# A fused attention and feed-forward block: q, k and v of the self-attention from three float32r products in place of one in fp32

## What is computed

```python
def _L0_attn_ref(x, w_qkv, b_qkv, w_out, b_out):
    B, T, C = x.shape                      # 64, 64, 256
    qkv = x @ w_qkv + b_qkv                # w_qkv is 256 x 768
    q, k, v = jnp.split(qkv, 3, axis=-1)
    ...
    att = jnp.einsum('bhqd,bhkd->bhqk', q, k) / jnp.sqrt(jnp.float32(D_HEAD))
    att = jnp.where(causal, att, -jnp.inf)
    att = jax.nn.softmax(att, axis=-1)
    y = jnp.einsum('bhqk,bhkd->bhqd', att, v)
    ...
    return y @ w_out + b_out

x = x + _L0_xattn_ref(_layernorm(x), ctx_1024, ctx_1024, ...)
x = x + _L0_attn_ref(_layernorm(x), w_qkv, b_qkv, w_out, b_out)
x = x + _L0_ffn_ref(_layernorm(x), w_gate, w_up, w_down)
```

## Time and profile before

| | |
|---|---|
| median of 3 runs | 1038.72 us (1038.37 to 1040.5) |
| the profiled execution | 1037.98 us |
| its span, first to last instruction | 1036.2 us |
| mean granted clock of PE | 0.98 |
| busy: PE, DVE, ACT, POOL | 89%, 80%, 70%, 37% |

### The profile page before, as it was taken

The page is one execution under the profiler, slowest core; times in us unless marked ns, Lnnn a source line. Parts: engine busy times, 40 slices in busy tenths (PEclk is TensorE's granted clock), DMA queues, the critical chain, the costliest instruction groups (busy, mean ns, idle before and its releaser), DMA issues. The chain is left out here.

```text
span 1036.2 us, 30640 instructions
## 1 busy us (share of the span) xinstructions
PE 919.6 (89%) x9794; PEld 737.1 (71%) x9794; DVE 831.3 (80%) x1810; ACT 728.0 (70%) x2061; POOL 386.4 (37%) x420
## 2 busy tenths in 40 slices
PE   4999999999999999999998799999999666666666
PEld 4888888888888888888887586777777433443444
DVE  4778787878787878787877588888888779999995
ACT  3676767676767676767676577767667378888886
POOL 2223232323232323232322445554554245445543
PEclk9899999999999999999999999999999779999999
DMA  8111111111111111111110000000000000000000
GB/s 278 43 35 40 35 40 35 40 35 40 35 40 35 40 35 40 35 40 35 40 35 1 2 2 1 0 0 0 0 0 1 1 1 21 25 20 20 20 25 31
DMA packets 31591, 31.36 MB, mean 30 GB/s; under 512 B 3280, under 2 KB 30800, under 8 KB 31568
## 3 DMA queue, kind: packets, MB, share of 16 engines
q1 hardware_dynamic: 30720, 30.73, 9.6%
q10 hardware_dynamic: 848, 0.33, 0.1%
HBM read 26.86 MB, written 4.19 MB: 30 GB/s over the span
## 5 line engine op out<-in xcount | busy, mean ns | idle before, releaser
L470 ACT ACTIVATE probs<-psum,nmax 128x256 f32<-128x256 f32 x512 | 237.6, 487 | 99.6 <-DVE nmax L430 99.6
L430 DVE TENSOR_REDUCE nmax<-psum 128x2 f32<-128x512 f32 x256 | 159.0, 684 | 31.0 <-PE psum L301 31.0
L478 POOL TENSOR_TENSOR rstd<-vare,minus_half 128x1 f32<-128x1 f32 x96 | 52.8, 550 | 337.0 <-DVE vare L368 337.0
L314 PE MATMUL psum<-id_sb,probs 128*128 128x128 f32 x1024 | 137.8, 278 | 10.5 <-ACT probs L470 8.9
L314 PEld LDWEIGHTS psum<-id_sb,probs 128*128 128x128 f32 x1024 | 113.8, 142 | 26.0 <-ACT probs L470 26.0
L487 POOL TENSOR_TENSOR cl<-c_sb,ch 128x512 fp32r<-128x512 f32 x64 | 81.2, 1269 | 104.3 <-ACT ch L445 104.3
L470 ACT ACTIVATION_READ_ACCUMULATOR probs<-psum,nmax 128x1 f32 x512 | 112.2, 219 | 0.0
L451 ACT ACTIVATE probsT<-psum 128x512 f32<-128x512 f32 x160 | 90.2, 608 | 13.5 <-PE psum L314 11.4
L494 POOL TENSOR_TENSOR rm<-rinv,hm_sb 128x256 f32<-128x256 f32 x64 | 39.8, 622 | 133.9 <-DVE rinv L407 133.9
L906 POOL TENSOR_TENSOR probs<-probs,silu 128x512 f32<-128x512 f32 x64 | 81.2, 1291 | 7.2 <-ACT probs L899 7.2
L378 DVE TENSOR_TENSOR v_sb<-psum,bv_sb 128x512 f32<-128x512 f32 x64 | 44.3, 692 | 39.6 <-PE psum L285 39.6
(11 more groups left out here) (117 smaller groups left out, 2318.2 us busy)
## 6 DMA issues: line engine op xcount, KB each, us to landing
c_sb<-in_ctx_t SPq DMA_DIRECT2D x64, 256.0 KB, 2.7
x_sb<-in_x SPq DMA_DIRECT2D x32, 128.0 KB, 2.1
out<-y_sb SPq DMA_DIRECT2D x32, 128.0 KB, 1.7
w_raw<-in_w_gate SPq DMA_DIRECT2D x1, 1024.0 KB, 7.9
w_raw<-in_w_up SPq DMA_DIRECT2D x1, 1024.0 KB, 10.0
w_raw<-in_w_down SPq DMA_DIRECT2D x1, 1024.0 KB, 12.5
wqkv_sb<-in_w_qkv SPq DMA_DIRECT2D x1, 768.0 KB, 6.5
wq_sb<-in_wq ACTq DMA_DIRECT2D x1, 256.0 KB, 4.2
```

The lines of the kernel that those rows point to most:

```text
L314: last = nc.tensor.transpose(sp[g][:, c:c + P], probs[:, 2 * g + u, kh * P:(kh + 1) * P], id_sb[:])
L430: nc.vector.tensor_reduce(nmax[:, 2 * g:2 * g + 2], sp[g].rearrange("p (u s) -> p u s", u=2), AX.X, ALU.max, negate=True).then_inc(max_don ...
L470: nc.scalar.activation(probs[:, j, :], sp[g][:, u * S:(u + 1) * S], ACT.Exp, bias=nmax[:, j:j + 1], accum_out=rsum[:, j:j + 1]).then_inc(e ...
```

## The change

The three float32r products replace the fp32 ones. The weights are split once, near the end of the cross-attention block: `wqkvh` by an ACT copy, `wqkvl` by a DVE subtraction. Each tile's transposed rows are split as they leave PSUM: ACT writes `xh` (in place of `xnT`, same shape), then DVE writes `xl`, PSUM less `xh`. `pe_qkv2` waits for `xl_done` and issues, for q and k, 24 matmuls in place of 8, and for v six in place of two. The next `pe_xt2` waits until `xl` has been read out of PSUM, the writing of `xh` and `xl` until the projections of the tile before are done (`v2_mm`).

Three things are moved or put in between. On PE `pe_xt2` of t + 3 goes from behind `pe_out2` to ahead of `pe_r2`. On ACT `act_xt2` goes from behind `act_r2` to ahead of it. On DVE `dve_xl` of t + 3 stands between `dve_sub2` and `dve_y2`.

```diff
@@ -78,7 +78,13 @@
         bk_sb = sb("bk_sb", [P, KT])
         bv_sb = sb("bv_sb", [P, D])
         bo_sb = sb("bo_sb", [P, D])
+
+
         wqkv_sb = sb("wqkv_sb", [P, KT, 3 * D])
+        wqkvh = sb("wqkvh", [P, KT, 3 * D], F32R)
+        wqkvl = sb("wqkvl", [P, KT, 3 * D], F32R)
+        xh = sb("xh", [P, KT, P], F32R)
+        xl = sb("xl", [P, KT, P], F32R)
         bqk_sb = sb("bqk_sb", [P, 2 * KT])
         bv2_sb = sb("bv2_sb", [P, D])
         wout_sb = sb("wout_sb", [P, KT, D])
@@ -514,7 +520,10 @@
         rstd2_done = sem("rstd2_done")
         xn2_done = sem("xn2_done")
         xt2_mm = sem("xt2_mm")
-        xt2_ev = sem("xt2_ev")
+        w2h_split = sem("w2h_split")
+        w2l_split = sem("w2l_split")
+        xh_done = sem("xh_done")
+        xl_done = sem("xl_done")
         qk_mm = sem("qk_mm")
         qk_ev = sem("qk_ev")
         v2_mm = sem("v2_mm")
@@ -595,21 +604,25 @@
         def pe_xt2(pe, t):
             pe.wait_ge(xn2_done, t + 1)
             pe.wait_ge(v2b_done, t)
+            pe.wait_ge(xl_done, t)
             for k in range(KT):
                 last = nc.tensor.transpose(xq_ps[:, k, :], xn[:, k * P:(k + 1) * P], id_sb[:])
             last.then_inc(xt2_mm, 1)
 
         def pe_qkv2(pe, t):
-            pe.wait_ge(xt2_ev, t + 1)
+            pe.wait_ge(xl_done, t + 1)
             pe.wait_ge(qk_ev, t * 4)
             for m in range(2 * KT):
+                cols = slice(m * P, (m + 1) * P)
+                for n, (w, x) in enumerate(((wqkvh, xh), (wqkvh, xl), (wqkvl, xh))):
+                    for k in range(KT):
+                        last = nc.tensor.matmul(qk_ps[:, m, :], w[:, k, cols], x[:, k, :],
+                                                start=n + k == 0, stop=n == 2 and k == KT - 1)
+            last.then_inc(qk_mm, 1)
+            for n, (x, w) in enumerate(((xh, wqkvh), (xh, wqkvl), (xl, wqkvh))):
                 for k in range(KT):
-                    last = nc.tensor.matmul(qk_ps[:, m, :], wqkv_sb[:, k, m * P:(m + 1) * P],
-                                            xnT[:, k, :], start=k == 0, stop=k == KT - 1)
-            last.then_inc(qk_mm, 1)
-            for k in range(KT):
-                last = nc.tensor.matmul(v2_ps, xnT[:, k, :], wqkv_sb[:, k, 2 * D:3 * D],
-                                        start=k == 0, stop=k == KT - 1)
+                    last = nc.tensor.matmul(v2_ps, x[:, k, :], w[:, k, 2 * D:3 * D],
+                                            start=n + k == 0, stop=n == 2 and k == KT - 1)
             last.then_inc(v2_mm, 1)
 
         def pe_scores2(pe, t, par):
@@ -678,6 +691,12 @@
 
         both = s_both.rearrange("p (a b) -> p a b", b=L)
 
+        def dve_xl(v, t):
+            v.wait_ge(xh_done, t + 1)
+            v.wait_ge(v2_mm, t)
+            nc.vector.tensor_tensor(xl[:], xq_ps, xh[:].bitcast(F32),
+                                    ALU.subtract).then_inc(xl_done, 1)
+
         def dve_max2(v, t):
             v.wait_ge(s2_mm, t + 1)
             nc.vector.tensor_reduce(nmax2[:], both, AX.X, ALU.max).then_inc(max2_done, 1)
@@ -717,7 +736,8 @@
 
         def act_xt2(a, t):
             a.wait_ge(xt2_mm, t + 1)
-            nc.scalar.activation(xnT[:], xq_ps, ACT.Copy).then_inc(xt2_ev, 1)
+            a.wait_ge(v2_mm, t)
+            nc.scalar.activation(xh[:], xq_ps, ACT.Copy).then_inc(xh_done, 1)
 
         def act_qk(a, t, par):
             a.wait_ge(qk_mm, t + 1)
@@ -1030,6 +1050,7 @@
                 body(NT - 1, False, True)
                 pe.wait_ge(w2_in, 16 * len(SET2))
                 pe.wait_ge(r_ev, NT * 2)
+                pe.wait_ge(w2l_split, 1)
                 pe_qkv2(pe, 0)
                 pe_out(pe, NT - 1, True)
 
@@ -1072,6 +1093,10 @@
                         v.wait_ge(y_ev, 1)
                         dve_stats(v, LN2, 0, at(0))
                         dve_xn(v, LN2, 0, at(0), xt2_mm)
+                    if last:
+                        v.wait_ge(w2h_split, 1)
+                        nc.vector.tensor_tensor(wqkvl[:], wqkv_sb[:], wqkvh[:].bitcast(F32),
+                                                ALU.subtract).then_inc(w2l_split, 1)
                     if not last:
                         dve_q(v, t + 1)
                     dve_o(v, t, 0)
@@ -1087,6 +1112,7 @@
                 with v.Fori(1, NT - 1) as t:
                     body(t, False, False)
                 body(NT - 1, False, True)
+                dve_xl(v, 0)
                 v.wait_ge(y_ev, 2)
                 dve_stats(v, LN2, 1, at(1))
                 dve_o(v, NT - 1, 1)
@@ -1108,6 +1134,9 @@
 
                 def body(t, last):
                     act_pt(a, t, 0)
+                    if last:
+                        a.wait_ge(w2_in, 16 * len(SET2))
+                        nc.scalar.activation(wqkvh[:], wqkv_sb[:], ACT.Copy).then_inc(w2h_split, 1)
                     if not last:
                         act_xt(a, t + 1)
                     if not last:
@@ -1179,11 +1208,11 @@
                     if wsum:
                         pe.wait_ge(wscale, 1)
                     pe_transpose2(pe, t)
+                    if ahead3:
+                        pe_xt2(pe, t + 3)
                     pe_r2(pe, t)
                     if not first:
                         pe_out2(pe, t - 1)
-                    if ahead3:
-                        pe_xt2(pe, t + 3)
                     pe_pv2(pe, t)
 
                 body(0, 0, first=True)
@@ -1205,6 +1234,7 @@
             def _(v):
                 v.wait_ge(w2_in, 16 * len(SET2))
                 dve_v2(v, 0, 0)
+                dve_xl(v, 1)
                 dve_stats(v, LN2, 2, at(2))
                 nc.vector.tensor_tensor(id2_b[:], id_sb[:, 0:L].unsqueeze(1).to_broadcast([P, 2, L]),
                                         id_sb[:, L:P].unsqueeze(1).to_broadcast([P, 2, L]),
@@ -1213,6 +1243,7 @@
                   .then_inc(b_set, 1)
                 dve_xn(v, LN2, 2, at(2), xt2_mm)
                 dve_v2(v, 1, 1)
+                dve_xl(v, 2)
                 dve_max2(v, 0)
                 dve_sub2(v, 0)
 
@@ -1233,6 +1264,8 @@
                         dve_max2(v, t + 1)
                     if ahead1:
                         dve_sub2(v, t + 1)
+                    if ahead3:
+                        dve_xl(v, t + 3)
                     if not first:
                         dve_y2(v, t - 1)
                     dve_o2(v, t)
@@ -1277,9 +1310,9 @@
                     if rounded is not None:
                         act_wround(a, rounded)
                     act_pt2(a, t)
-                    act_r2(a, t)
                     if ahead3:
                         act_xt2(a, t + 3)
+                    act_r2(a, t)
                     if ahead1:
                         act_exp2(a, t + 1)
                         act_v2(a, t + 1, 1 - par)
```

## The result

The changed kernel takes 1077.96 us (median of 4 runs, 1076.87 to 1079.79), the kernel before beside it 1038.55 (4 runs): a ratio of 1.0383, 95% interval 1.0356 to 1.0410. It is slower by 39 us, where 27 were forecast. The profiled execution took 1076.87 us, 1074.6 of it span, against 1036.2 before.

A forecast was written before the change was run, and what follows sets the result against it. The prediction took PE's own work to set the steady period. It summed 24 steady tiles at +0.82 us (+19.7) and +7.0 elsewhere to 26.7, added to the median 1038.72: 1065.5 us, range 1056 to 1078.

The forecast's parts named there:

- the price of a float32r matmul: q and k projections on PE: each 128-column matmul costs its weight load, 0.111 us; 24 loads for 16, +0.89 us a tile.
- the exposed load beside L571: PE, v matmuls to next L623: of two L571 loads, one has nothing to stream over it and costs 0.11 us.
- columns as the price: Rival for q and k: loads hide behind matmuls of 0.06 us, giving 1030 us, faster; chance 0.06.
- fp32 work below 256 columns: Rival for q and k: float32r there runs at the fp32 price, +3.4 us a tile, some 1143 us; chance 0.05.
- the wait at the rounding: Tile where DVE rounds a weight matrix before the scores' maximum: projections wait for `xl`, starting at 623.6 instead of 619.25.
- the wait for `xl`: Each steady tile: PE's next projections wait for DVE's subtraction, +0.10 us a tile, bounds 0 and 0.42.
- the copy of `r`: ACT, behind `xh`: ends about 2.4 us after the transposes start, pushing PE by less than 0.1.
- the edge terms: The seven tiles before the steady ones, and the end: +7.0 us in all; at half or half as much again, 3.5 either way.
- the turn behind the rounding: Period after the tile with DVE's weight rounding: PE's own 8.0 us in place of 9.1.
- the start up to tile 4: First self-attention tiles: +1.7 us by tile 2, then +0.7 in all up to tile 4.
- The upper bound: Top of the forecast range for the whole kernel, 1078 us; the range 1056 to 1078 had chance 0.80.
- From the last q and k block to the end: End of the kernel: the last projections, at 800.66, add +0.7 us.

The follow-up runs named there:

- the fill: Changed kernel plus 54 unused PE transposes: 12, 8 and 6 at the self-attention block's start, 28 behind turn 3; 1073.38 us, ratio 1.0327.
- the last fill: Changed kernel, ACT's `r` copy before `xh`, rounding after `xl`, 12, 8 and 6 unused transposes, 30 more before first p times v; 1062.37 us.

## Why the prediction was wrong in size and right in direction

**Right: the price of a float32r matmul.** "I therefore price a float32r matmul of 128 columns at its load, 0.111", from the exposed load beside L571. It is 0.112, and the experiments with half the columns (0.112) and half the weights (0.060) show it to be the load. q and k take 0.85 us more (forecast 0.89), v 0.11 less (forecast 0.17); q, k, v and scores up to the transposes take 4.92 us, 4.90 by the sum. The rivals of columns as the price and of fp32 work below 256 columns both fall.

**Right: the wait at the rounding.** The turn that was forecast at 11.5 (7.14 + 4.35) is 11.56.

**Mis-sized: "+0.10 us a tile" for the wait for `xl`.** It is 0.26. PE starts 0.14 behind the end of `xl`, which in place of "right behind it" costs 0.09. And "the copy of `r`" does not stay "inside the wait for `xl`": the copy ends at 2.33 behind the transposes (729.07 against 726.74), about where the sum had it (2.4), but the p times v matmuls start only 0.24 later, at 2.57, where the sum had them start with the copy's end. So the wait that the profile shows in each steady turn isn't the one for `xl`, but this (640 to 820; total us, times, longest):

```profile
PE psum L678 <- ACT r_sb L765: 3.8, 22, 0.2
```

In every second turn, where the loop ends, they push the next projections to 3.33 behind the transposes; in the others these start at 3.19, which is `xl`. That is 0.07 on average. 24 x (0.09 + 0.07) = 3.8 of the 4.2 us in the steady turns.

**Failed: the clock in the edge terms.** The prediction said of a block at the lower clock that "the columns bind and half as many passes a matmul make up for the longer block". They don't: there the float32r matmuls are 0.214 apart, twice 0.111 within 4%, and with half the columns still 0.214, so the loads bind there too, and the block costs about half as much again as the fp32 one at either clock. And it took the stretches at the lower clock between the start of the stage and the steady tiles as they were before, 3.4 us, where the changed kernel has 13.7 + 6.8 = 20.5. This is the term that failed: the turn behind the rounding was to give back 1.1 us and took 2.1 more, and of these 3.2 the fill shows 3.06 to be clock; the start up to tile 4 took 5.6 - 1.3 = 4.3 in place of 2.4, and with the clock whole there (the last fill, which has the other mends too) the turns from tile 3 to 7 are 8.0, 8.47, 8.08 and 8.85.

**The upper bound.** 1078 held "the edge terms at half as much again", 3.5 us, and 0.117 a load. Nothing in it stood for the clock, though the prediction named a lower clock among the things that would make it wrong. With the measured ratio on the median that the sum was added to, 1038.72 x 1.0383 = 1078.5, the time lies just above, by less than the interval of the ratio (1075.7 to 1081.3). Which side of the bound it fell on is chance; that it is 13 us above the sum isn't. The 3.06 us of the stretch at 630 alone, as a term with both ends, would have covered it.

**Open.** From the last q and k block to the end after takes 2.8 us more, forecast 0.7. In the float32r kernels here it is between 234.8 and 238.4, and the clock varies there; no run here takes these 2 us apart. The cause of the stretch at 582.4 stays open in part. It goes away when the idle time ahead of it (1.37 and 0.93 us) is filled, but also with half the weights, where the same waits stay: neither the waits nor the 24 full loads alone bring it about.

## What to carry to other kernels

Price a TensorE matmul by the larger of its weight load and its columns: with 128 moving columns three float32r products are 24 loads against 16, and cost more than fp32; with 256 they are cheaper, so the tiling has to change with the type. A new wait on PE costs its length and can cost the lower clock behind it (3.06 us behind a wait of 3.31 here): look up the granted clock in the windows around each new idle time, and forecast it as a term of its own. Compare two kernels at a place ahead of the edit as well: here up to 4.7 us came and went there between kernels whose code was the same. Where PE newly depends on an engine, look for long work ahead of that step in the engine's queue, and put it behind; a PE wait that can't be removed may be worth filling with work that nobody reads.

## What the hardware showed that I had not expected

- A weight load slows with the granted clock: 0.112 us a float32r matmul at 1.00, 0.214 at 0.50; with half the weights 0.060 and 0.107.
- After the same waits of 1.37 and 0.93 us at the start of the block the clock was at 0.50 for very different times in kernels that differ in what PE does behind them: not at all with half the weights, for 3.4 us with 256 columns, for 10.2 to 17.1 us with the 24 full loads.
- Less streaming can cost time: with 64 of 128 columns in the q and k matmuls, and everything else the same, the clock fell to 0.50 in 16 of the 24 steady turns, mostly for 3.4 us, and the kernel got 23 us slower.
- Transposes that nothing reads keep the clock up: with 54 of them the changed kernel took 4.6 us less (0.6% by the two ratios), and with 30 and the later rounding the kernel before took 4.6 us less (2.6 to 6.5); the traces show 1.8 and 2.5 of these at the places of the edits. Each stands in the trace as one record with a load of 140 ns, where an fp32 matmul is two records. The Trainium skill ("TensorE: Matmul & The Clock Gate", "Part 4: PE-mode transpose") says that transposes don't count as busy work for the clock in the same way; here the clock stood at 1.00 behind them, where it had been 0.50.
- DVE's end to PE's start across a semaphore is 0.14 us.
